# Long attention of a gated cross-attention stack: one burst of weighted sums per batch behind all its scores, and the first tile maxima taken in one instruction each

## What is computed

```python
q_r = jnp.einsum('bshq,hqr->bhsr', q_big, W_qr)
k_r = jnp.einsum('bld,hdr->bhlr', kv_r, W_kr)
scores = jnp.einsum('bhsr,bhlr->bhsl', q_r, k_r)
attn = jax.nn.softmax(scores, axis=-1)
ctx_c = jnp.einsum('bhsl,bld->bhsd', attn, kv_r)
```

## Time and profile before

| | us |
|---|---|
| median of 3 runs | 2622.87 (2621.98 to 2623.61) |
| the profiled execution, time | 2621.18 |
| the profiled execution, span of its instructions | 2619.4 |
| of which layer 1's long attention, first maximum to last row sum | 611.6 to 1045.5 |

### The profile page before, as it was taken

One profiled execution on the slowest core, in us unless ns is written; L12 is line 12 of the kernel. 1 busy time (PEld: TensorE's weight loads), 2 busy tenths in 40 slices (PEclk: granted clock), 3 DMA queues, 4 the chain that ended last, 5 costly groups with the idle time before them and its releaser, 6 DMA issues. The chain is left out here.

```text
span 2619.4 us, 33757 instructions
## 1 busy us (share of the span) xinstructions
PE 2382.8 (91%) x11268; PEld 1695.7 (65%) x11268; DVE 1616.8 (62%) x2686; ACT 979.4 (37%) x1461; POOL 814.2 (31%) x485
## 2 busy tenths in 40 slices
PE   7787779988999999599899999989899999995998
PEld 4676669974665665476466665589555665655997
DVE  3545544427777776668777777531477777754444
ACT  3223134423444444121244444411424444532443
POOL 0223023300444444036244454410124444421332
PEclk9555789977999999789799999979879999997999
DMA  2334164306434340312343433049453434302332
GB/s 40 95 109 130 59 178 157 104 19 192 97 86 107 90 104 21 114 40 85 90 104 84 113 91 92 21 149 370 151 133 80 116 88 95 89 8 60 117 117 86
DMA packets 110749, 267.27 MB, mean 102 GB/s; under 512 B 26035, under 2 KB 62813, under 8 KB 106690
## 3 DMA queue, kind: packets, MB, share of 16 engines
q1 hardware_dynamic: 109954, 263.87, 36.7%
q0 software_dynamic: 672, 1.84, 0.2%
HBM read 219.08 MB, written 46.41 MB: 101 GB/s over the span
## 5 line engine op out<-in xcount | busy, mean ns | idle before, releaser
L1207 DVE TENSOR_REDUCE keep_top<-banks 128x1 f32<-128x500 f32 x1008 | 656.6, 676 | 269.4 <-PE banks L1146 264.5
L1265 ACT ACTIVATE att_ex<-banks 125x896 f32<-125x896 f32 x576 | 526.4, 918 | 260.4 <-PE banks L1135 238.7
L1315 POOL TENSOR_TENSOR att_acc<-att_acc,att_two 125x896 f32<-125x896 f32 x186 | 393.4, 2115 | 447.9 <-DVE att_two L1222 434.0
L1163 PE MATMUL banks<-att_ex,att_v 125*64 125x448 f32 x2304 | 464.7, 545 | 0.0
L1146 PE MATMUL banks<-keep_kh,keep_qt 128*128 128x500 f32 x1008 | 393.2, 439 | 17.4 <-DVE keep_top L1207 6.9
L1222 DVE TENSOR_TENSOR att_two<-att_ex 125x896 f32<-125x896 f32 x288 | 316.1, 1136 | 48.2 <-ACT att_ex L1265 47.8
L1135 PE MATMUL banks<-keep_qt,keep_kh 128*125 128x448 f32 x1152 | 333.5, 371 | 2.3 <-ACT att_ex L1265 2.3
L1135 PE MATMUL banks<-att_qm,att_kl 65*125 65x448 f32 x1152 | 331.8, 369 | 0.0
L1163 PEld LDWEIGHTS banks<-att_ex,att_v 125*64 125x64 f32 x2304 | 152.5, 136 | 247.9 <-issue 200.9
L1593 PE MATMUL banks<-moe_xs,moe_w 128*128 128x448 f32 x1272 | 280.1, 370 | 24.0 <-DVE moe_xs L1708 23.2
L1146 PEld LDWEIGHTS banks<-keep_kh,keep_qt 128*128 128x128 f32 x1008 | 188.1, 197 | 174.9 <-issue 85.7
(11 more groups left out here) (240 smaller groups left out, 2585.2 us busy)
## 6 DMA issues: line engine op xcount, KB each, us to landing
keep_kh<-kvt_hi SPq DMA_DIRECT2D x96, 375.0 KB, 5.1
q_rows<-mats_q SPq DMA_DIRECT2D x24, 896.0 KB, 4.2
keep_qt<-q_rows SPq DMA_DIRECT2D x48, 448.0 KB, 6.4
moe_raw<-L_experts_dram SPq DMA_DIRECT2D x53, 384.0 KB, 4.2
att_kl<-kvt_lo SPq DMA_DIRECT2D x48, 375.0 KB, 8.2
att_v<-kvn SPq DMA_DIRECT2D x24, 720.0 KB
sort_wu<-L_experts_dram SPq DMA_DIRECT2D x14, 1024.0 KB, 9.4
moe_cb<-comb_rows SPq DMA_DIRECT2D x62, 224.0 KB
```

What stands on the lines that cost most here:

```text
L1163: last = pe.matmul(PS[WEIGHED][64 * e:64 * e + 64, 0:HALF], v[:, s // 2, u, s % 2, :], ex[:, u % RING, e, :], start=u == 0, stop=u == UNIT ...
L1207: dve.tensor_reduce(top[:, s % 2, n // NS, n % NS:n % NS + 1], PS[6 + (PIECES * s + n) % 2][:, 0:SB], AX.X, ALU.max).then_inc(mx_done, 1)
L1265: act.activation(ex[:, u % RING], scored, ACT.Exp).then_inc(exp_done, 1)
L1315: pool.tensor_tensor(a, two[:, 0] if n == 1 else a, two[:, n % 3], ALU.add).then_inc(gathered, 1)
```

## The change

`ex` keeps all 12 units of a batch. On PE a batch is now: three rounds of scores with maxima and no `weigh` between them, `turn` after the second round, then `sums` of the batch before, then `weigh` for all 12 units in one run. On DVE the six pairs of a batch come after its third round of maxima, and `invert` behind them. On ACT `row_sums` follows the last exponential. On POOL `place` of the batch before follows all five gathers. On SP `shifts` of the next batch moves ahead of `sums` and `scales`. The exponential of unit u now waits for the `weigh` and the pair of the same unit in the batch before. At a layer's start the three pieces of a tile go into three neighbouring banks, and one DVE instruction takes the maximum of 128 x 1500 with its sign turned, straight into `nm`; two sets of three banks take turns.

```diff
-        ex = st.sb("ex", [KP, RING, 2, HALF])
+        ex = st.sb("ex", [KP, UNITS, 2, HALF])
...
+                    if b < B - 1:
+                        shifts(b + 1)
                     if b:
                         sums(b - 1)
                         scales(b - 1)
-                    if b < B - 1:
-                        shifts(b + 1)
...
                 def turn(s, b):
                     pe.wait_ge(nm_ready, b + 1)
-                    if not known(b, 2):
-                        pe.wait_ge(sm_done, b - 1)
+                    if not known(b, 3):
+                        pe.wait_ge(sm_done, b - 2)
...
                 def batch(s, b, left):
...
-                        for u in range(4 * i, 4 * i + 4):
-                            weigh(s, b, u)
-                        if i == 0 and not known(b, 1):
-                            pe.wait_ge(gathered, GATHERS * b)
-                            pe.wait_ge(high_done, b + 1)
-                            sums([acc[:, (s + 1) % 2]])
                         if i == 1 and left:
                             turn((s + 1) % 4, b + 1)
-
-                for n in range(PIECES):
-                    top_scores(0, 0, n)
+                    if not known(b, 1):
+                        pe.wait_ge(gathered, GATHERS * b)
+                        pe.wait_ge(high_done, b + 2 if left else b + 1)
+                        sums([acc[:, (s + 1) % 2]])
+                    for u in range(UNITS):
+                        weigh(s, b, u)
+
+                pe.wait_ge(qk_in[0], 48 + (l - 1) * B // 4 * 48)
+                for t in range(NT):
+                    if t >= 2:
+                        pe.wait_ge(mx_done, NS * (t - 1))
+                    for c in range(NS):
+                        last = pe.matmul(PS[t % 2 * NS + c][:, 0:SB], q[:, 0, 128 * t:128 * t + 128],
+                                         kh[:, 0, SB * c:SB * c + SB], start=True, stop=True)
+                    last.then_inc(mx_ready, NS)
...
                         if i == 1 and left:
                             shift((s + 1) % 4, b + 1)
-                        pair(b, 2 * i)
-                        pair(b, 2 * i + 1)
-                        if i == 1 and not known(b, 1):
-                            invert(s + 1, b - 1)
-
-                for n in range(PIECES):
-                    tops(0, 0, n)
-                shift(0, 0)
+                    for p in range(PAIRS):
+                        pair(b, p)
+                    if not known(b, 1):
+                        invert(s + 1, b - 1)
+
+                for t in range(NT):
+                    dve.wait_ge(mx_ready, NS * t + NS)
+                    a = t % 2 * NS * 512
+                    scored = PS.all[:, a:a + NS * 512].rearrange("p (c k) -> p c k", c=NS)[:, :, 0:SB]
+                    dve.tensor_reduce(nm[:, 0, t:t + 1], scored, AX.XY, ALU.max, negate=True).then_inc(mx_done, NS)
...
-                        act.wait_ge(pv_done, UNITS * b + u - RING + 1)
-                        act.wait_ge(paired, PAIRS * b + (u - RING) // 2 + 1)
+                        act.wait_ge(pv_done, UNITS * (b - 1) + u + 1)
+                        act.wait_ge(paired, PAIRS * (b - 1) + u // 2 + 1)
...
                     for n in range(1, PAIRS if b < B - 1 else PAIRS - 2):
                         gather(b, n)
-                        if n == 3 and b:
-                            place(b - 1)
+                    if b:
+                        place(b - 1)
```

More of the change, by code:

```diff
@@ L40 @@
 PAIRS = UNITS // 2
-RING = 4
+ROUND = 4
 PIECES = NS * NT
@@ L1163, in weigh @@
                         last = pe.matmul(PS[WEIGHED][64 * e:64 * e + 64, 0:HALF], v[:, s // 2, u, s % 2, :],
-                                         ex[:, u % RING, e, :], start=u == 0, stop=u == UNITS - 1)
+                                         ex[:, u, e, :], start=u == 0, stop=u == UNITS - 1)
                     last.then_inc(pv_done, 1)
@@ L1175, in batch @@
                 def batch(s, b, left):
-                    for i in range(UNITS // 4):
-                        for slot in range(5):
+                    for i in range(UNITS // ROUND):
+                        for slot in range(ROUND + 1):
                             if slot:
-                                scores(s, b, 4 * i + slot - 1)
+                                scores(s, b, ROUND * i + slot - 1)
                             for ahead, n in pieces(i, slot, left):
                                 top_scores((s + ahead) % 4, b + ahead, n)
-                        for u in range(4 * i, 4 * i + 4):
-                            weigh(s, b, u)
-                        if i == 0 and not known(b, 1):
-                            pe.wait_ge(gathered, GATHERS * b)
-                            pe.wait_ge(high_done, b + 1)
-                            sums([acc[:, (s + 1) % 2]])
                         if i == 1 and left:
                             turn((s + 1) % 4, b + 1)
-                for n in range(PIECES):
-                    top_scores(0, 0, n)
+                    if not known(b, 1):
[12 more added lines that the diff above has]
+                    last.then_inc(mx_ready, NS)
                 turn(0, 0)
@@ L1220, in pair @@
                         dve.wait_ge(gathered, GATHERS * b - GATHERS + p + 3)
-                    a = 2 * p % RING
-                    dve.tensor_tensor(two[:, p % 3], ex[:, a], ex[:, a + 1], ALU.add).then_inc(paired, 1)
+                    dve.tensor_tensor(two[:, p % 3], ex[:, 2 * p], ex[:, 2 * p + 1], ALU.add).then_inc(paired, 1)
                 def invert(s, b):
@@ L1236, in batch @@
                             shift((s + 1) % 4, b + 1)
-                        pair(b, 2 * i)
-                        pair(b, 2 * i + 1)
-                        if i == 1 and not known(b, 1):
-                            invert(s + 1, b - 1)
-                for n in range(PIECES):
-                    tops(0, 0, n)
-                shift(0, 0)
+                    for p in range(PAIRS):
[7 more added lines that the diff above has]
+                    dve.tensor_reduce(nm[:, 0, t:t + 1], scored, AX.XY, ALU.max, negate=True).then_inc(mx_done, NS)
+                dve.wait_ge(mx_done, PIECES)
+                dve.engine_nop().then_inc(nm_ready, 1)
                 for n in range(NT):
@@ L1259, in exps @@
                     act.wait_ge(st_ready, UNITS * b + u + 1)
-                    if not (known(b, 1) and u < RING):
-                        act.wait_ge(pv_done, UNITS * b + u - RING + 1)
-                        act.wait_ge(paired, PAIRS * b + (u - RING) // 2 + 1)
+                    if not known(b, 1):
+                        act.wait_ge(pv_done, UNITS * (b - 1) + u + 1)
+                        act.wait_ge(paired, PAIRS * (b - 1) + u // 2 + 1)
                     a = 2 * (u % 2)
                     scored = PS.all[0:KP, a * 512:a * 512 + 1024].rearrange("p (e k) -> p e k", e=2)[:, :, 0:HALF]
-                    act.activation(ex[:, u % RING], scored, ACT.Exp).then_inc(exp_done, 1)
+                    act.activation(ex[:, u], scored, ACT.Exp).then_inc(exp_done, 1)
                 def numerators(s, b):
@@ L1286, in batch @@
                 def batch(s, b, left):
-                    for i in range(UNITS // 4):
-                        for u in range(4 * i, 4 * i + 4):
+                    for i in range(UNITS // ROUND):
+                        for u in range(ROUND * i, ROUND * i + ROUND):
                             exps(b, u)
-                        if i == 0 and not known(b, 1):
-                            row_sums(b - 1)
                         if i == 1 and left:
                             high((s + 1) % 4, b + 1)
+                    if not known(b, 1):
+                        row_sums(b - 1)
                     if left:
```

## The result

The changed kernel takes 2716.8 us in the median (2713.92 to 2717.89), the kernel before 2623.0: a ratio of 1.0356, 95% interval 1.0338 to 1.0374. It is 3.6% slower; the forecast was slower, 2705 us in a range of 2665 to 2795. The profiled execution has 2713.92 us, its span 2712.1.

A forecast was written before the change was run, and what follows sets the result against it. PE was taken as the bound, with weighted sums covering slower work. Per layer -3.3 + 14 x 2.08 + 1.4 + 0.1 = +27.3, three layers +82, giving 2705 us in a range of 2665 to 2795.

The forecast's parts named there:

- Seams: Between rounds on PE: without weighted sums as cover they cost 0.5 and 0.9 us; PE alone ends a batch at 27.2.
- Pairs: At the batch's end on DVE: pairs and gathers exclude each other, chain 10.35 us, DVE 0.6 late, batch 27.8 us.
- Key loads: On SP: starting 3.1 us into the batch, the loads land at 10.7 against the need at 12.1, hidden.
- C: Key loads land late, at 13.0 us into the batch: 0.9 us a batch, 2743 us; chance 0.07.
- E: PE's gaps lower its clock for a third of each batch: some 4 us each, near 2870 us; chance 0.04.
- Rival B: At the batch's end gather 3 beats pair 5: 2.1 us more in 42 batches, 2793 us; chance 0.18.
- Start: At a layer's start, one maximum over 1500 columns takes 1.73 us; 13.6 us instead of 16.9, gain 3.3.
- Batch 14: The batch without a third round of maxima: 26.0 us against 24.6, +1.4 a layer.
- Rival D: At the two seams, maxima running ahead save 0.23 us each and add nothing: -11 a layer, 2590 us; chance 0.04.

The follow-up runs named there:

- late gathers: Changed kernel with GpSimd's gathers behind all six pair sums, five buffers for pairs and the accumulator as sixth: 2675.9 us, ratio 1.0214.
- later scales: Changed kernel with SyncE's inverse row sums one batch later, behind the next key and query loads: 2708.4 us, ratio 1.034.
- transpose in the burst: Changed kernel with the shifts' transpose behind the fourth weighted sum, its copy and load moved later: 2699.0 us, ratio 1.0311; with late gathers 2662.6 us, 1.0148.

## Why the prediction was right

**Seams.** I had the second step of the second round at 6.05 from the batch's start, the transpose at 11.83, the seventh step of the third round at 16.90 and the end at 27.2. In the kernel with late gathers, which shows them undisturbed, they are at 5.88, 11.75, 16.83 and 27.09. The model of two banks (0.43 to DVE's start, 0.68, 0.18 back to PE) was taken from the earlier trace rows and carries 14 x 1.37 = 19 of the 25 to 26 us that each of the first two layers lost. The idle times there were put too high, 0.8 and 1.2 where 0.55 and 0.98 stand.

**Pairs.** The chain of six pairs was put at 10.35 and measures 1506.52 - 1496.18 = 10.34, with the order that I gave it: pair 3 behind gather 1, pair 5 ahead of gather 3. DVE is 0.6 late as forecast, but PE gets only about 0.4 of it: 0.17 as a wait behind the burst, and 0.44 in all by the fourth step of maxima (2.86 from the batch's start against 2.42 with late gathers). The batch is 27.5 instead of 27.8, and this term was too large by 0.3 in 42 batches, 12.6 us.

**Key loads and clock**, the rivals C and E. Here the forecast was wrong: it called the key loads hidden and the clock untouched, and priced both at nothing. I had both as alternatives, each by itself, with chances of 0.07 and 0.04. They came together and in few batches: loads start 3.75 into the batch, not 3.1, since I had counted DVE's 0.6 to the batch before; they land after 10.3 at worst where I had 8.7; and where PE waited over 0.8 us for them the clock fell. Three batches by this and one by B in layer 3: 31.60 + 31.06 + 31.27 + 29.98 - 4 x 27.55 = 13.7 us, and layer 3 is 12.4 longer than the others. Taken together C and E have a price of 3.3 us per such load, (31.60 + 31.06 + 29.98) / 3 - 27.55; I had priced C at the wait alone and E at 4 us in every batch. Elsewhere in the loops of this profile the clock stays at 1.00: neither the 0.55 nor the 0.98 at the seams lowers it by itself. E's stall of some 18% of a batch follows from no sum in the forecast; its own 0.8, 1.2 and 0.6 make 9%, and the three waits measured make 1.7 of 27.48 us, 6%.

**Rival B** happened once in this profile, and once in each of the other two that keep this order (later scales, transpose in the burst): gather 3 ahead of pair 5, 3.7 us more with the clock in this one, not 2.1.

**Start.** Gain 2.6, 3.3 and 3.4 us for 3.3; the long reduction takes 1.71 to 1.72 for 1.73. **Batch 14** 26.46 - 24.58 = +1.9, where I had +1.4: the same 0.4 from the pairs, which I had left out there. With late gathers it is 25.94, against my 26.0.

**Sum**: forecast +82, measured +92.7 in the profiled executions, 10.8 more: +13.7 for the outliers of layer 3, -12.6 for the pairs, +2.4 for the first distance of each layer (28.3), +2 for four batches at 27.9 to 28.2, +1.5 for the batches 14, +0.7 for the starts, and 2.8 lie outside the attention layers, which I do not explain. The 28.3 went with the late gathers and so belongs to pairs and gathers; why the first is the longest stays open.

That 2705 came within 12 us of 2716.8 is in part luck: the pairs that were priced 12.6 too high nearly cancel the outliers of 13.7 that were priced at nothing. What the forecast earned is the direction, the cost of the seams and the course of the pairs.

**Rival D**, that the burst can be faster, was wrong for this kernel and right about what it could be: it said that maxima which never make PE wait would save 0.23 at each of two seams, 0.5 a batch, and asked for a third bank. No third bank was needed; another order of the same maxima, with late gathers and the transpose in the burst, did it, and the batch is 0.34 under before.

## What to carry to other kernels

Work that fills a gap also hides how slow the engine beside it is. Before bundling it, list what waits at each place where it stood, here two PSUM banks and a chain of maximum, shift and transpose. If the bundle is wanted, change the producers' order with it: alternate the counts so that the slower reader never has two bursts in a row, and put two-input adds of DVE and of GpSimd at different times. Look at what else a moved wait frees or delays: the later scales cured the loads and sent `place` into the pairs. And test the parts of a change apart: one of the two here was a gain of 0.3% all along.

## What the runs showed of the hardware

- A DVE add and a GpSimd add over SBUF run one after the other, whole instruction by whole instruction, and the one that comes second counts as busy while it waits (a gather 2.87 for 2.1, a pair 2.74 for 1.03 at 2095.99). The Trainium skill ("SBUF — State Buffer", Who interferes with whom) says that the two exclude each other, and these traces agree with those two numbers. The holes of 1.98 between the pairs are something else, the wait for a buffer, and only longer by the 0.8 that the gather lost. Of two that become free at the same moment, pair 5 and gather 3, nearly always DVE went first, and not always: pair 5 lost at 2095.99, once in this profile.
- DVE reads of PSUM (the maxima, 0.65 us each) ran beside gathers at their usual pace: 11.08 us for five in the kernel with late gathers and the transpose in the burst, where nine maxima lay beside them.
- A single wait of TensorE can cost more behind it than in it. At waits of 1.10, 1.80, 0.86 and 2.33 us the granted clock fell to half, for nearly 7 us the first time and for 3 to 4 us the others. On top of the wait it cost some 1.4 to 3 us each. The first three of these waits came 0.3 us behind the 0.98 at the transpose. In the run with the transpose in the burst, where no such wait stands ahead, it fell at waits of 1.56, 1.66, 1.85, 2.48 and 3.20, and did not at 1.54, 1.63, 2.01 and 2.39. So the length of the wait alone does not decide, and what does the runs do not show.
